# Two of eight batch-norm statistics moved to earlier links of VectorE's rstd chain, in a one-core GNN layer

## The reference: what is computed

```python
h   = maximum(layernorm(x), 0)
agg = segment_sum(edge_attr, src, num_segments=50000)
z   = silu(concatenate([h, agg], -1) @ W1 + b1) @ W2 + b2
out = x + ((z - mean(z)) * rsqrt(var(z) + eps) * gamma + beta) + h
```

## Time and profile before

| | before |
|---|---|
| runs, us | 783.76, 780.91, 779.41 (median 780.91) |
| the profiled execution, us | 779.33 |
| its span, us | 777.7 |
| granted TensorE clock, mean | 0.987 |
| busy: PE, PE weight load, DVE, ACT, POOL | 92%, 76%, 91%, 81%, 63% |
| instructions on DVE | 2275 |
| bn_stats (L823) | 392, 281 ns each as recorded |

### The profile page before, as it was taken

One profiled execution on the slowest core, in us unless ns is written; L12 is line 12 of the kernel. 1 busy time (PEld: TensorE's weight loads), 2 busy tenths in 40 slices (PEclk: granted clock), 3 DMA queues, 4 the chain that ended last, 5 costly groups with the idle time before them and its releaser, 6 DMA issues.

```text
span 777.7 us, 15386 instructions
## 1 busy us (share of the span) xinstructions
PE 719.1 (92%) x4554; PEld 594.4 (76%) x4554; DVE 706.2 (91%) x2275; ACT 629.1 (81%) x2034; POOL 488.9 (63%) x414
## 2 busy tenths in 40 slices
PE   7999998789999999999999999999999999999994
PEld 3555546668888888888888888888888888888883
DVE  8999997889898989898989898989898989898988
ACT  7999975568878788788887887888878887878793
POOL 3000017567877777777787777777877777777730
PEclk9999999799999999999999999999999999999997
DMA  5000000123332323232323232323332323222112
GB/s 201 1 2 1 2 4 23 46 73 104 102 104 103 103 104 102 103 105 101 103 102 104 101 102 99 106 101 103 104 102 101 103 102 106 103 91 80 50 65 78
DMA packets 28265, 65.89 MB, mean 85 GB/s; under 512 B 8473, under 2 KB 10028, under 8 KB 28180
## 3 DMA queue, kind: packets, MB, share of 16 engines
q1 hardware_dynamic: 15604, 51.90, 18.0%
q0 software_dynamic: 12576, 12.99, 6.6%
HBM read 52.05 MB, written 25.60 MB: 100 GB/s over the span
## 4 chain that ended last, share of the span: by engine, by line
DVE 33%; issue 33%; PE 13%; another core or an unknown queue 13%; ACT 6%; DVEq 0%
DVE stat L823 9%; DVE T L1034 7%; PE y L657 4%; ACT hi L548 4%; DVE lo L1022 2%; PE za L652 2%; PE pre L652 2%; PE za L645 2%; PE pre L645 2%; DVE R L1029 1%; DVE var L863 1%; DVE R L1004 1%; DVE guess L867 1%; ACT hi L546 1%
## 5 line engine op out<-in xcount | busy, mean ns | idle before, releaser
L435 POOL DMA_INDIRECT G<-in_edge_attr_dram,slot_edge x388 | 478.6, 1234 | 152.6 <-issue 110.3
L740 PEld LDWEIGHTS y<-w2c,S 128*128 128x128 f32 (+1 forms) x1556 | 189.9, 193 | 10.8 <-issue 2.8
L740 PE MATMUL y<-w2c,S 128*128 128x128 f32 (+1 forms) x1556 | 191.1, 276 | 2.1 <-ACT S L555 2.1
L1022 DVE TENSOR_TENSOR lo<-za,hi 128x1024 fp32r<-128x1024 f32 (+1 forms) x98 | 119.0, 1214 | 60.0 <-ACT hi L548 53.4
L538 ACT ACTIVATE H<-X,shift,rstd 128x128 f32<-128x128 f32 x392 | 163.8, 513 | 2.9 <-DVE shift L882 2.4
L715 PE MATMUL pre<-hi,w1h 128*128 128x512 f32 (+1 forms) x392 | 163.4, 417 | 2.3 <-issue 1.2
L716 PE MATMUL pre<-hi,w1l 128*128 128x512 f32 (+1 forms) x392 | 154.8, 395 | 0.4 <-issue 0.4
L555 ACT ACTIVATE S<-pre,b1c 128x512 f32<-128x512 f32 (+1 forms) x196 | 128.5, 731 | 12.0 <-remote 8.7
L720 PE MATMUL pre<-lo,w1h 128*128 128x512 f32 (+1 forms) x392 | 123.2, 395 | 0.2
L546 ACT CAST hi<-za 128x512 fp32r<-128x512 f32 (+1 forms) x98 | 59.5, 607 | 71.0 <-remote 67.7
L701 PE MATMUL za<-HOT,G 128*128 128x128 f32 (+1 forms) x784 | 104.8, 277 | 1.8 <-issue 1.1
(11 more groups left out here) (154 smaller groups left out, 1005.5 us busy)
## 6 DMA issues: line engine op xcount, KB each, us to landing
X<-in_x_dram SPq DMA_DIRECT2D x48, 512.0 KB
out_dram<-R SPq DMA_DIRECT2D x48, 512.0 KB
G<-in_edge_attr_dram,slot_edge POOLq DMA_INDIRECT x388
X<-in_x_dram SPq DMA_DIRECT2D x1, 424.0 KB
out_dram<-R SPq DMA_DIRECT2D x2, 192.0 KB
w1f<-in_L_gnn_W_dram SPq DMA_DIRECT2D x1, 256.0 KB
w2f<-in_L_gnn_W_dram SPq DMA_DIRECT2D x1, 128.0 KB
srci<-in_src_dram SPq DMA_DIRECT2D x1, 85.8 KB
```

Source lines behind the costliest of these rows:

```text
L435: nc.gpsimd.indirect_dma_start(G[b.j][:, t, :], None, source, bass.IndirectOffsetOnAxis(ap=slot_edge[:, bass.ds(b.number(TILES, t), 1)], a ...
L740: done = nc.tensor.matmul(places[t][0:r], S[c][:, m, t * r:(t + 1) * r], w2c[:, m, :], start=False, stop=True, skip_group_check=True)
L1022: nc.vector.tensor_tensor(out=lo[c][:, :, w], in0=za[:, :, w], in1=hi[c][:, :, w].bitcast(F32), op=ALU.subtract).then_inc(lo_done, 1)
```

## The change

A table says at which place each of the eight statistics stands. Statistic 0 goes from place 3 to place 1, in front of `x + beta`; statistic 1 from place 4 to place 2, in front of `H0 + R`; statistics 2 to 5 move up to places 3 to 6; statistics 6 and 7 stand at places 8 and 9. Places 7 and 10 hold nothing. No instruction is added or taken away.

```diff
+    STATISTICS_AT = {1: (0,), 2: (1,), 3: (2,), 4: (3,), 5: (4,), 6: (5,), 8: (6,), 9: (7,)}
...
                     if place == 0 and b.plus(-1).exists(NB) and b.n > 2:
                         one_hots(b.plus(-1))
-                    if 3 <= place < 3 + TILES and b.plus(1).exists(NB) and b.n > 3:
-                        statistics(b.plus(1), place - 3)
+                    if b.plus(1).exists(NB) and b.n > 3:
+                        for t in STATISTICS_AT.get(place, ()):
+                            statistics(b.plus(1), t)
                     if b.plus(-3).exists(NB):
                         if place == 1:
                             x_plus_beta(b.plus(-3))
```

## The result

| | before | after |
|---|---|---|
| median of 4 runs, us | 780.16 (778.84 to 783.76) | 771.93 (769.50 to 773.30) |
| profiled execution, its span, us | 779.33, 777.7 | 771.46, 769.9 |

The ratio is 0.9884, with a 95% interval of 0.9841 to 0.9927. In the kernel after, a line up to L823 of before stands one further down; the calls in `powers` (from L855), `x_plus_beta`, `residual`, `one_hots` and `split_low` stand two further down, so `lo` is L1024.

What follows compares the result with a forecast made beforehand. It took a ring of waits through VectorE's `powers`, PE and ACT as the bound. Growth of 0.25 us over 44 chains, 11.0 us, on the median of 780.91 gave 791.9 us; range 779.5 to 795.5.

Steps and rivals of the forecast that it cites:

- the chain: VectorE's dependent tiny instructions in `powers`, with statistics between: forecast to grow from 2.23 to 2.48 us, `lo` to `lo` 7.33 to 7.58.
- covered pairs: In VectorE's `powers`, a tiny instruction followed by a statistic that hides its wait: six at 0.279 us, together 1.67.
- a statistic in front of an add: Places 1 and 2 of `powers`, where 1024-column adds already hide the wait: each statistic adds its full 0.195 us, together 0.39.
- bare links: Places 7 and 10 of `powers`, dependent tiny instructions with no statistic between: two at 0.209 us, together 0.42.
- The drain rule: Rival for VectorE's `powers`: bare links cost nothing more, 2.23 us stays, time 780.9 us; chance 3%.
- The parts set at nothing: Later `x + beta`, `H0 + R`, gathers, load of x, `rstd` and `shift`, statistic 0's earlier wait, unchanged DMA order: cost 0.
- I take 0.25: Price per step, chosen between 0 and 0.25 us: VectorE's whole growth reaches the step, 11.0 us over 44 chains; chance 50%.
- the ring as the rows show it: Closed waits from VectorE's `lo` and `powers` over PE's transposes and ACT's `hi` to the next `lo`: 12.85 us, setting the step.
- the 2.42 us: Time between the recorded end of PE's transposes and ACT's `hi` waiting for them; the prediction called this link not understood.
- partly swallowed: Rival: half of the growth in VectorE's `powers` comes through, 0.12 x 44 = 5.5 us, time about 786 us; chance 10%.
- the handover shortens: Rival at PE to ACT: PE idling longer before its transposes gets signals through sooner, time about 770 us; chance 7%.
- Swallowed at the handover: Rival at PE to ACT: `hi` follows PE's second layer's end, so later `lo` costs 0, about 781 us; chance 25%.

Runs made afterwards that it cites:

- the delay alone: Kernel before plus three tiny VectorE instructions that nobody reads, behind `shift` in front of the second `lo`: 778.74 us, ratio 0.9981.

## Why the prediction was wrong

**What held.** Each term of the chain: covered pairs 0.28 for 0.279, a statistic in front of an add 0.20 to 0.21 for 0.195, bare links 0.19 for 0.209, the chain 7.57 for 7.58. The drain rule of the Trainium skill (VectorE: DVE Perf Modes, "The DRAIN you can't avoid"), by which a semaphore in a chain costs nothing extra and the chain would have stayed at 2.23, does not hold for these instructions: the same number of instructions on VectorE took 0.24 us more in each step, and without gathers the kernel 5.35 us more. The parts set at nothing showed no cost: in the trace no new wait stands at `statistics`, and no term is missing in the chain. The gathers did move against PE's work, though (0.10 us ahead of the second layer's end in short steps, 0.54 in the long one shown, 0.41 before), and what that is worth stays open.

**What failed, first.** The step "I take 0.25", every link of the ring moves. It rests on "Nearest is the ring as the rows show it: PE waits for this `lo` in each step". PE does wait for it, but what sets the step is the other ring, from the second layer's end over `hi`, silu and `layer1` to the next second layer's end (3.66 + 4.36 + 4.82 = 12.84 us), and the chain is not in it. With the chain longer by the same 0.24 us and nothing else changed, the step went from 12.87 to 12.90 only, and the time to 0.9981 of before. The link in question was the handover from PE to ACT. It was drawn with a constant length, though the text said that nothing showed what filled the 2.42 us. ACT waited there for 71.0 us in all, more than PE or VectorE at any link of the ring, and it was treated as a fixed duration while the sum dealt in hundredths. Measured, it is 2.38 us in one step and hidden behind ACT's own work in the next, and 0.04 us on other chips or without gathers. That the long steps came to 13.05, beside the 13.10 of the forecast, is luck: PE idles 0.43 us in them, where 0.86 was forecast, and such a step comes only behind a short one.

**What failed, second.** The price was about twice too high even where the chain does count. Of the chain's 0.24 us, 0.12 fell into slack in front of the next `lo` ("I take 0.25. Over 44 chains that is 11.0 us."). Where no signal is late, the step grew by 0.13 (5.35 us without gathers, 6.09 with them on the other kind of chip). That is almost the figure of the rival "partly swallowed" (0.12 x 44 = 5.5), by luck: it named no mechanism, and it was meant for the kernel with late signals.

**The rivals.** That the handover shortens (7%, 770 us) is what happened, and its figure was near. Its mechanism, that a PE idling longer gets its signals through sooner, is not what the runs show: with PE idle for the same 0.86 us and VectorE's order unchanged there is no gain (the delay alone, 778.74), and with PE idle for 0.64 there is one of 1.9% (765.58). So the nearness of the figure is luck. Its evidence was weak too, as the prediction itself said ("another wait took over"). In the odd step at 308 the first `hi` came early, but the second one paid for it, as ACT's timeline of the kernel before has it:

```profile
309.63 0.58 ACT L546 CAST hi<-za 128x512 fp32r<-128x512 f32 x1
313.05 0.59 ACT L548 CAST hi<-za 128x512 fp32r<-128x512 f32 x1 [2.84 <-remote]
```

That step is one of the longest, 14.18 us. `lo` waits for the second `hi`, and that is the one to follow. "Swallowed at the handover" (25%) described the delay alone: `hi` follows something that runs from the end of PE's second layer, VectorE's wait falls, and the step stays within 0.03 us.

**What stays open.** Why PE's signals are late beside gathers, and which part of the change makes every other handover shorter: the delay does not, the side of the adds on which the statistics stand does not matter, and the gather's place has an effect of which the size and the sign in the sum were not settled. So the gain of the change is traced to its place and not to its cause. Nor was it found what differs between the two kinds of chips. The change itself ran on the slower kind alone; what it would do on the other is taken from the kernel with the statistics behind the adds, whose chain has its length.

On the slower kind of chip the change is ahead by 6.9 to 8.2 us in three comparisons (ratios 0.9884, 0.9905, 0.9904), on the faster kind the kernel with the statistics behind the adds is behind by 6.1.

## What to carry to other kernels

An idle time whose releaser the profile can't name is a term of its own, and not a constant: before costing a change of 0.25 us beside a wait of 2.4 us, find out what the wait hangs on, by leaving the suspected engine's work out once. Differences along one path always add up to the step, so a closed sum does not show that a ring binds; look for a second ring that closes without the changed link (here over ACT's silu), and for slack in front of each link, before a price is carried through whole. A gain that comes from an unexplained wait can be the property of some chips; time it on several before it is kept.

## What the runs showed of the hardware

- **Signals from PE that come late only beside gathers, and only on some of the chips tried.** `hi` starts 2.42 us behind the recorded end of the transposes with gathers, 0.04 without them, and 0.04 with them on other chips. One and the same kernel takes 780 us in the one case and 722 in the other, 8%; the granted clock is 1.00 in each of these steps.
- **The handover has preferred lengths.** With the same work a step of the change took either 12.46 or 13.05 us, alternating over most of the loop, and its three profiled runs show it alike (20, 21 and 20 short steps of 44).
- **A short dependent instruction on VectorE** starts 0.19 to 0.21 us behind the one it reads when nothing stands between. An independent one starts 0.08 behind it, so with a statistic of 0.20 between, the pair takes 0.28 and the wait costs nothing.
- **A memset of one column on POOL** between two gathers cost nothing: it took 0.12 of a gap of 0.3 us that is there anyway. One of 384 columns took 0.43 us.
